# A four-part transformer kernel: last stage rearranged, and unread matrix products in the waits of the matrix engine

## The chip, the core and the metric

The kernel runs on one core of one Trainium2 chip. It is one program with an instruction stream for each engine: TensorE (PE) for matrix products, VectorE (DVE) and ScalarE (ACT) for elementwise work, GpSimd (POOL) for elementwise work and for scattering rows by indirect DMA, and SyncE (SP) for issuing the other DMAs. The engines run beside each other and are held together by semaphores alone. The metric is the device time of one execution in microseconds (us): the median over several.

## What is computed

An input x of 2 x 2048 tokens with 512 features, all float32, passes four residual blocks, each ahead of it with a layer norm without weights:

```python
x = x + rope_attention(norm(x), context)            # cross attention, 16 heads of 64, tanh-capped scores, 128 keys
x = x + quantised_ffn(norm(x))                      # weights and activations rounded to 8 bits; scale = max|x| over the whole tensor
x = x + masked_attention(norm(x), context)          # 16 heads of 32, 128 keys, masked scores set to 1e-9
x = x + routed_experts(norm(x))
def routed_experts(x):
    probs = softmax(x @ Wg + bg)                    # 512 columns
    idx = argmax(probs); p = max(probs); e = idx % 8
    return relu(x @ We[e] + be[e]) * p              # one of 8 experts for each token
```

The FFN needs the largest magnitude of its whole input before it can round the first value, and that of its whole hidden tensor before the product with w_down.

## The kernel before

The 4096 tokens are 32 tiles of 128 rows, in 8 groups (chunks) of 4 tiles (TPC = 4). x stays in SBUF as `xres`, 32 tiles of 512 float32. A float32 product is made as three products of rounded parts: hi x hi, lo x hi and hi x lo, where hi is the value rounded to a shorter float and lo = value - hi. Rounding to hi is ACT's, the subtraction for lo is DVE's (POOL's for the expert weights).

**Start of the rope attention (L441 to L600).** DVE normalises the context as soon as it has landed (L524 to L532), PE turns it (L580), ACT applies gain and shift (L491), and PE multiplies it with the key weights (L588). DVE rotates the results (L546 to L551) with a table that comes by DMA.

**Into the quantised stage.** The last products of the attention are followed by 44 transposes of weights in bf16 (L217). DVE finds the largest normalised magnitude (L921 to L1015), PE spreads it over the partitions with one product (L1209), DVE makes scales of it (L1017 to L1026), ACT scales x (L1285), DVE rounds (L1318, L1320), PE transposes (L1354) and makes the first small gate and up products (L1362), then the large ones (L1380).

**Down block.** Again a peak (DVE L1479, PE L1545, DVE L1481 to L1485), then ACT scales the hidden tensor (L1457) and DVE rounds it (L1493, L1495), in pieces (the lists FIRST, A_PIECE and D_PIECE), and PE multiplies (L1548).

**Masked attention (`first_step` and `body`, L2050 to L2120).** A written order of DVE's steps: `x_low` (L1971, low part of a turned row), `take_tops` (L1986, maxima of the scores, ahead of ACT's exponentials), `mask_scores` (L1980), `norm_row` (L1965), `invert` (L1996), `attn_low` (L2006), and in the last step `gate_top` (L2612 to L2617), the best of the 512 router columns. `gate_constants` (L2589 to L2597) sets small tables for the router. In tile 0 of a step PE's order is set by `first_step`.

**Routed experts (class ExpertStage, from L2360).** t counts tiles: t = 0 to 31 are router tiles (GATES = 32), t = 32 to 70 are slots (SLOT_TILES = 39), j = t - 32. For a router tile PE turns the normalised row (L2782), ACT rounds it (L2539) and DVE takes the low part (L2603, `take_lo`), PE makes 12 products with the router weights (L2792 to L2794), DVE finds the best column (L2612, L2614), ACT sums exponentials (L2545), and at the end of a group `hot` makes a one-hot of the experts (L2622 to L2629), PE ranks the tokens (L2805 to L2815) and `places` turns ranks into row numbers (L2634 to L2640). POOL's `scatter_rows` (L2486, L2493) writes the group's 4 tiles to DRAM sorted by expert. When 6 groups (EARLY) are counted, `tile_count` (L2646 to L2657), `tile_ends` (L2662 to L2668) and `tile_table` (L2678 to L2691) say which expert and which row each of the first 17 slots has (FULL_TILES); after all 8 groups the same is made for the other 22. For a slot, SP loads 128 sorted rows (L2434, `load`; 8 buffers; from j = 4 on after scatter(6)), PE turns them and makes 12 products with the expert's weights (L2835 to L2837), DVE adds the bias (`add_bias`, L2729) and applies relu, probability and residual (`finish`, L2733 to L2737), and POOL's `scatter_out` (L2500) writes the rows back by token. The weights of the 8 experts come early; ACT rounds them (`weights_high`, L2551), one 128 x 512 piece at a time, 4 for each expert, in the tiles that `pieces` names; the buffer of the rounded ones is that of x in part, so that a piece of group g waits for scatter(g). POOL makes their low parts (`weights_low`, L2478, L2484). In POOL's list, two low parts of expert e stand ahead of scatter(e - 1), two behind. Rows of sorted tiles that no token fills are written by SP (L2441, L2447).

Each engine takes its own instructions strictly in the written order: DVE's order within a tile t is add_bias of the slot before, take_lo of the next tile, finish, places, and then whatever extra work the list assigns to that t.

## Time and profile before

| | |
|---|---|
| median of 3 executions | 1476.54 us (1476.39 to 1477.39) |
| profiled execution | 1474.24 us |
| its span, first to last instruction | 1472.4 us |
| PE busy | 1416.4 us, 96% |
| DVE busy | 1194.5 us, 81% |
| ACT busy | 863.6 us, 59% |
| POOL busy | 524.1 us, 36% |
| mean granted clock of TensorE | 0.992 |

Busy is the time in which an engine had an instruction of its own under way. The granted clock is given as a share of the full 2.4 GHz; 0.50 is 1.2 GHz. In rows of the timeline, "x4" stands for four instructions in a row that are shown as one, and the bracket gives the time for which the engine was idle before, with the instruction or DMA that ended the wait. "issue" means that nothing in the profile explains it. A float32 product of 128 columns is two records.

### The profile page before, as it was taken

What the parts mean: (1) busy time and instruction counts of PE and PEld (TensorE: products, weight loads), DVE (VectorE), ACT (ScalarE), POOL (GpSimd) and SP (SyncE); (2) the same over time, 40 slices, a digit from 0 to 9 for tenths busy, and PEclk for the clock granted to TensorE, in tenths of its full rate; (3) what the DMA queues carried; (4) which work ended last, traced back from release to release, by engine and by line L of the source; (5) the groups of instructions that cost most, each with busy time, mean ns of one, the idle gap of its engine ahead of it and who ended that gap; (6) DMA issues with size and microseconds to landing.
All of it is one profiled execution on the core that took longest, in us unless ns stands there. A gap on an engine that the chain in (4) does not pass through costs nothing. (4 is left out here: it accounts for less than half of the span.)

```text
span 1472.4 us, 30141 instructions
## 1 busy us (share of the span) xinstructions
PE 1416.4 (96%) x10478; PEld 1061.3 (72%) x10478; DVE 1194.5 (81%) x2582; ACT 863.6 (59%) x2056; POOL 524.1 (36%) x511
## 2 busy tenths in 40 slices
PE   7999999999999999899998999999999999998996
PEld 5777777777777777644443467888888877776885
DVE  6778888787887865589988969999999997786775
ACT  2544444444444444655547848999999886773432
POOL 0122222222222222200003747655656655764333
PEclk9999999999999999999999999999999999999999
DMA  8511111110111102134415710000000026226641
GB/s 302 187 48 46 46 46 46 46 42 8 38 37 37 53 8 79 30 104 177 166 64 233 303 42 3 4 2 3 3 3 4 4 87 229 87 92 201 192 155 54
DMA packets 68658, 122.03 MB, mean 83 GB/s; under 512 B 30398, under 2 KB 36926, under 8 KB 67008
## 3 DMA queue, kind: packets, MB, share of 16 engines
q1 hardware_dynamic: 62864, 103.71, 20.8%
q0 software_dynamic: 5680, 16.85, 2.9%
q8 instruction: 66, 1.08, 0.3%
q14 instruction: 48, 0.39, 0.1%
HBM read 77.46 MB, written 39.80 MB: 80 GB/s over the span
## 5 line engine op out<-in xcount | busy, mean ns | idle before, releaser
L1840 ACT ACTIVATE c_probs<-c_score,c_minus_top 128x128 f32<-128x128 f32 x512 | 181.2, 381 | 27.2 <-DVE c_minus_top L1986 24.8
L1778 POOL TENSOR_TENSOR c_probs<-c_probs,c_recip 128x512 f32<-128x512 f32 x128 | 140.5, 1101 | 128.8 <-DVE c_recip L1996 125.1
L700 POOL TENSOR_TENSOR a_attn_lo_parts<-a_attn,a_attn_hi_parts 128x512 fp32r<-128x512 f32 x64 | 80.6, 1293 | 200.5 <-ACT a_attn_hi_parts L762 200.5
L758 ACT COPY a_attn<-a_pv_ps 128x512 f32<-128x512 f32 x64 | 36.6, 572 | 145.3 <-PE a_pv_ps L1068 145.3
L1451 POOL TENSOR_TENSOR xres<-xres,b_delta 128x512 f32<-128x512 f32 x24 | 48.3, 2028 | 196.9 <-DVE b_delta L1508 196.9
L1840 ACT ACTIVATION_READ_ACCUMULATOR c_probs<-c_score,c_minus_top 128x1 f32 x512 | 113.0, 221 | 0.0
L430 PE MATMUL a_bank<-a_x_hi_parts,a_wq_hi 128*128 128x256 f32 x512 | 106.4, 289 | 0.4 <-PEq L445 0.3
L696 POOL TENSOR_TENSOR a_x_lo_parts<-a_x_full,a_x_hi_parts 128x512 fp32r<-128x512 f32 x30 | 38.0, 1290 | 192.9 <-ACT a_x_hi_parts L733 192.9
L430 PE MATMUL a_bank<-a_x_lo_parts,a_wq_hi 128*128 128x256 f32 x512 | 102.3, 281 | 0.0
L430 PE MATMUL a_bank<-a_x_hi_parts,a_wq_lo 128*128 128x256 f32 x512 | 102.2, 281 | 0.0
L727 ACT ACTIVATE a_x_full<-a_bank,a_shift,a_gain 128x256 f32<-128x256 f32 x60 | 30.2, 555 | 119.4 <-PE a_bank L422 119.4
L1036 PE MATMUL a_bank<-a_wo_hi,a_attn_hi_parts 128*128 128x512 f32 x248 | 99.4, 401 | 0.0
L1038 PE MATMUL a_bank<-a_wo_hi,a_attn_lo_parts 128*128 128x512 f32 x248 | 98.1, 396 | 0.0
L1037 PE MATMUL a_bank<-a_wo_lo,a_attn_hi_parts 128*128 128x512 f32 x248 | 98.0, 395 | 0.0
L2539 ACT CAST d_xT_hi<-c_score 128x512 fp32r<-128x512 f32 x67 | 39.3, 586 | 98.2 <-PE c_score L2782 90.1
L1304 ACT ACTIVATE b_silu<-b_gate,ahead_scale 128x512 f32<-128x512 f32 x88 | 60.2, 684 | 61.7 <-PE b_gate L1380 61.1
L742 ACT ACTIVATE a_probs<-a_score_ps 128x1024 f32<-128x1024 f32 x64 | 65.6, 1025 | 41.2 <-PE a_score_ps L1053 41.2
L1380 PE MATMUL b_up<-b_xT,ahead_upT 128*128 128x512 bf16 x348 | 89.3, 379 | 0.0
L1380 PE MATMUL b_gate<-b_xT,ahead_gateT 128*128 128x512 bf16 x348 | 89.3, 379 | 0.0
L1980 DVE COPY_PREDICATED_SCALAR c_score<-c_masks,c_tiny 128x512 f32 (+1 forms) x96 | 89.1, 928 | 0.0
L430 PEld LDWEIGHTS a_bank<-a_x_hi_parts,a_wq_hi 128*128 128x128 f32 x512 | 78.3, 188 | 14.2 <-issue 6.3
L1986 DVE TENSOR_REDUCE c_minus_top<-c_score 128x4 f32<-128x512 f32 (+1 forms) x96 | 83.4, 869 | 3.2
(352 smaller groups left out, 4234.2 us busy)
## 6 DMA issues: line engine op xcount, KB each, us to landing
hidden<-b_hidden SPq DMA_DIRECT2D x5, 2816.0 KB, 8.3
b_hidden<-hidden SPq DMA_DIRECT2D x5, 2816.0 KB, 11.9
xres<-in_x SPq DMA_DIRECT2D x8, 1024.0 KB, 14.2
d_we<-in_we SPq DMA_DIRECT2D x8, 1024.0 KB, 6.7
xres<-in_w_gate_up SPq DMA_DIRECT2D x7, 1024.0 KB, 5.3
d_got<-rows SPq DMA_DIRECT2D x20, 258.0 KB, 2.9
xres<-rows SPq DMA_DIRECT2D x19, 258.0 KB, 2.7
a_rot<-in_rot SPq DMA_DIRECT2D x16, 256.0 KB, 3.0
```

The lines of the kernel that those rows point to most:

```text
L430: last = nc.tensor.matmul(out[:, i, :], w[:, k, cols], x[:, k, :], start=(j == 0 and i == 0), stop=(j == len(products) - 1 and i == 1))
L700: nc.gpsimd.tensor_tensor(of_spread(attn_lo, g), of_spread(attn, g), of_spread(attn_hi, g), ALU.subtract).then_inc(attn_lo_ready, 1)
L742: nc.scalar.activation(buf, score_ps[:, p % 2], ACT.Tanh, scale=1.0 / (DH0 ** 0.5 * GROK)).then_inc(capped, 1)
L1036: nc.tensor.matmul(out, hi, w_hi, start=first, stop=False)
L1037: nc.tensor.matmul(out, hi, w_lo, start=False, stop=False)
L1038: return nc.tensor.matmul(out, lo, w_hi, start=False, stop=last)
L1304: nc.scalar.activation(silu[:, u % RING, :], gate_ps[:, u % RING, :], ACT.Silu, scale=gate_scale[:, i:i + 1]).then_inc(silu_ready, 1)
L1380: last = nc.tensor.matmul(ps[:, u % RING, :], w[:, k, i * P:(i + 1) * P], xT[:, n % 2, k, :], start=(k == 0), stop=(k == KB - 1))
L1778: nc.gpsimd.tensor_tensor(part, part, recip[:, t % 2, heads].unsqueeze(2).to_broadcast([P, QUADS, KEYS]), ALU.mult).then_inc(scaled, 1)
L1840: last = nc.scalar.activation(probs[:, t, at, :], score_ps[:, h, g, :], ACT.Exp, bias=minus_top[:, h, g:g + 1], accum_out=total[:, t, at:a ...
L1980: ch.step(nc.vector.copy_predicated(part, masks[:, j, t, :].unsqueeze(1).to_broadcast(shape), tiny[:].unsqueeze(2).to_broadcast(shape)))
L1986: nc.vector.tensor_reduce(minus_top[:, PIECES[i]].rearrange("p h g -> p (h g)"), part, AX.X, ALU.max, negate=True).then_inc(top_ready, 1)
```

## The change

A helper `keep_busy` issues products of 128 x 128 float32 whose results nobody reads; it is called at ten places of PE's list. In the masked attention `gate_constants` moves into the first step, and in tiles with a gate `norm_row` moves behind `gate_top`. In ExpertStage POOL scatters a group's rows ahead of the low parts of the next expert; the two last low parts of the last expert go to DVE; the last group's four scatters are issued one by one behind the outputs of slots 4 to 7; counting takes three operations instead of five, and the tables are cut into `tile_passed`, `tile_experts` and `tile_rows`, spread over more tiles; SP fills unused rows later; the last slot is made in two halves of 256 columns. Cut to its core:

```diff
+
+
+def keep_busy(nc, out, square, times):
+
+    for _ in range(times):
+        nc.tensor.matmul(out, square, square, start=True, stop=True)
...
+            zeros, zeros_set = ctxT[:, 0, 0:P], sem("zeros_set")
+                    nc.vector.memset(zeros, 0.0).then_inc(zeros_set, 1)
+                    pe.wait_ge(zeros_set, 1)
+                    keep_busy(nc, ring.at(0)[:, 0, 0:P], zeros, 21)
...
+                pe.wait_ge(freed["dve"], last_out.emptied[1])
+                keep_busy(nc, peak_bank[:, 1, 0:P], ident[:], 4)
                 pe.wait_ge(ahead.peak_ready, 1)
-                pe.wait_ge(freed["dve"], last_out.emptied[1])
                 nc.tensor.matmul(peak_bank[:, 0, 0:P], row_scale[:, 0:1].to_broadcast([P, P]), ident[:], start=True, stop=True).then_inc(ahead.peak_turned, 1)
+                pe.wait_ge(ahead.taken, ahead.GROUPS_AHEAD + 1)
+                keep_busy(nc, score_ps[:].rearrange("p u h c -> p (u h c)")[:, 0:P], ident[:], 7)
...
+                    keep_busy(nc, up_ps[:, RING - 1, 0:P], ident[:], 11)
                     turn_first(0)
                     for t in range(1, TPC):
...
+                    pe.wait_ge(silu_ready, CHUNKS * IT - 2)
+                    keep_busy(nc, gate_ps[:, (CHUNKS * IT - 3) % RING, 0:P], ident[:], 6)
...
+                    keep_busy(nc, out_ps[:, BANKS - 2, 0:P], ident[:], 6)
                     pe.wait_ge(peak_ready, 1)
...
+                    keep_busy(nc, out_ps[:, BANKS - 2, 0:P], ident[:], 7)
                     pe.wait_ge(ld_down, 16 * KB)
...
+                                if q == 1 and t == 0 and i == A_PIECE.start:
+                                    keep_busy(nc, out_ps[:, g, 0:P], ident[:], 4)
                                 if t == 0 and i == A_PIECE.start:
                                     pe.wait_ge(whole_by_act, q)
...
+                    pe.wait_ge(out_freed, TPC * (CHUNKS - 1) - BANKS + TPC + 1)
+                    keep_busy(nc, out_ps[:, (TPC * (CHUNKS - 1) - BANKS + TPC) % BANKS, 0:P], ident[:], 5)
...
                     find_tops(1, 0, 1, 0)
                     find_tops(1, 0, 1, 1)
                     mask_scores(1, 0, 1, 2)
+                    gate_constants()
                     x_low(2 * NT, 0, 0, use(0, 0, 0, "T").out)
                     take_tops(2)
                     invert(1, 1, 0)
...
                         second = isinstance(n, int) and tile == 1
-                        if second:
-                            gate_constants()
...
-                        if s["N"]:
+                        if s["N"] and "L" not in s:
                             norm_row(tile + 2 * NT + 1, (t + 1) % 2)
                         if "L" in s:
                             dve.wait_ge(bank_full, gate_use[t].full)
                             gate_top(t)
+                            if s["N"]:
+                                norm_row(tile + 2 * NT + 1, (t + 1) % 2)
...
+        FILL = G + 3
+        LAST_SLOT, HALVES = SLOT_TILES - 1, (slice(0, D // 2), slice(D // 2, D))
...
+            if t // TPC == 2:
+                return {0: (), 1: (), 2: (0, 1), 3: (2, 3)}[t % TPC]
             return {0: (), 1: (0, 1), 2: (2,), 3: (3,)}[t % TPC]
...
+                sp.wait_ge(scattered, 16 * TPC * 2)
                 sp.dma_start(be[:].rearrange("p e n -> p (e n)"), io["be"].partition_broadcast(P)).then_inc(ld_be, 16)
                 for j in range(G):
                     load(j)
-                sp.wait_ge(no_row_set, 2)
-                sp.dma_start(io["rows"][NO_ROW:NO_ROW + P, :], no_token[:]).then_inc(filled, 16)
-                sp.wait_ge(behind_ready, 1)
                 for j in range(G, SLOT_TILES):
                     load(j)
-                    if j - G < EXPERTS:
-                        first = sp.value_load(behind_u[0:1, j - G:j - G + 1], min_val=0, max_val=NO_ROW - P)
-                        sp.dma_start(io["rows"][bass.ds(first, P), :], no_token[:]).then_inc(filled, 16)
+                    if j == FILL:
+                        sp.wait_ge(no_row_set, 2)
+                        sp.dma_start(io["rows"][NO_ROW:NO_ROW + P, :], no_token[:]).then_inc(filled, 16)
+                        sp.wait_ge(behind_ready, 1)
+                    for e in range(2 * (j - FILL), 2 * (j - FILL) + 2):
+                        if 0 <= e < EXPERTS:
...
-                if e >= 1 and k < 2:
+                if e >= 1 and k < 2 and e != EARLY:
                     pool.wait_ge(out_full, done(TPC * e))
-                elif e >= 1:
+                elif 1 <= e < EXPERTS - 1:
                     pool.wait_ge(hot_ready, e + 1)
                 nc.gpsimd.tensor_tensor(we_lo[:, e, k], we[:, e, k], we_hi[:, e, k], ALU.subtract).then_inc(we_lo_ready, 1)
...
-                for e in range(1, EXPERTS):
-                    for k in range(2):
+                for e in range(1, EXPERTS - 1):
+                    scatter_rows(e - 1)
+                    for k in range(KB):
                         weights_low(e, k)
-                    scatter_rows(e - 1)
-                    for k in range(2, KB):
-                        weights_low(e, k)
-                scatter_rows(GROUPS - 1)
+                for k in range(2):
+                    weights_low(EXPERTS - 1, k)
+                scatter_rows(GROUPS - 2)
                 for j in range(SLOT_TILES):
                     scatter_out(j)
+                    if TPC <= j < 2 * TPC:
+                        scatter_rows(GROUPS - 1, range(j - TPC, j - TPC + 1))
...
-                        for k in pieces(t):
+                        for k in pieces(t) if t < GATES - 2 else ((2, 3), ())[t - GATES + 2]:
                             weights_high(t // TPC, k)
...
-                ch.step(nc.vector.tensor_copy(counts[:], counted(i)))
-                ch.wait()
-                ch.step(nc.vector.tensor_scalar(whole[:], counts[:], float(add), None, ALU.add))
-                ch.wait()
-                ch.step(nc.vector.tensor_copy(whole_i[:], whole[:]))
+                ch.step(nc.vector.tensor_scalar(whole_i[:], counted(i), float(add), None, ALU.add))
...
-                    return x.unsqueeze(1).to_broadcast([1, n, EXPERTS])
                 dve.wait_ge(rstd_ready, len(DEVIATIONS))
                 ch.wait()
-                ch.step(nc.vector.tensor_tensor(passed[:, 0:n], each(ends[:]), place.unsqueeze(2).to_broadcast([1, n, EXPERTS]), ALU.is_le))
+                ch.step(nc.vector.tensor_tensor(passed[:, 0:n], ends[:].unsqueeze(1).to_broadcast([1, n, EXPERTS]),
+                                                place.unsqueeze(2).to_broadcast([1, n, EXPERTS]), ALU.is_le))
 
+            def tile_experts(j0, n):
+                ch.step(nc.vector.tensor_scalar(tile_expert[:, j0:j0 + n], expert_of[:, 0:n], float(EXPERTS - 1), None, ALU.min))
+
+            def tile_rows(j0, n):
-                ch.step(nc.vector.tensor_copy(tile_expert[:, j0:j0 + n], expert_of[:, 0:n]))
+                ch.step(nc.vector.scalar_tensor_tensor(row_of[:, 0:n], row_of[:, 0:n], origin[:, 0:1], ahead.table("slot", 1)[:, 0:n], ALU.add, ALU.add))
                 ch.wait()
-                ch.step(nc.vector.tensor_scalar(row_of[:, 0:n], row_of[:, 0:n], float(NO_ROW), None, ALU.min))
+                nc.vector.tensor_scalar(tile_row[:, j0:j0 + n], row_of[:, 0:n], float(NO_ROW), None, ALU.min).then_inc(tables_ready, 1)
+            def early_ends():
+                tile_ends(whole[0:1], ahead.table("first_row", 1))
+
+            def early_taken():
+
+                first = ahead.table("first_row", 1)
                 ch.wait()
...
             def rows_behind():
-                ch.step(nc.vector.tensor_tensor(behind[:], counts[0:1], ahead.table("first_row", 1), ALU.add))
-                ch.wait()
-                nc.vector.tensor_copy(behind_u[:], behind[:]).then_inc(behind_ready, 1)
+                nc.vector.tensor_tensor(behind_u[:], counted(1)[0:1], ahead.table("first_row", 1), ALU.add).then_inc(behind_ready, 1)
...
+            def last_low():
+                for k in range(2, KB):
+                    at = EXPERTS - 1, k
+                    dve.wait_ge(we_hi_ready, KB * EXPERTS - KB + k + 1)
+                    nc.vector.tensor_tensor(we_lo[:, at[0], k], we[:, at[0], k], we_hi[:, at[0], k], ALU.subtract).then_inc(constants, 1)
+
+            def expert_number(j):
+                return dve.value_load(tile_expert[0:1, j:j + 1], min_val=0, max_val=EXPERTS - 1)
...
                     if t == TPC * EARLY + 1:
                         tile_count(0, 0)
                     if t == TPC * EARLY + 2:
                         early_ends()
+                        tile_passed(FULL_TILES)
                     if t == TPC * EARLY + 3:
-                        tile_table(0, FULL_TILES)
-                    if t == GATES + 1:
+                        tile_experts(0, FULL_TILES)
+                        tile_rows(0, FULL_TILES)
+                    if t == GATES - 1:
+                        last_low()
+                    if t == GATES + 2:
+                        early_taken()
+                    if t == GATES + 3:
                         no_row()
-                    if t == GATES + 2:
+                    if t == GATES + 4:
                         tile_count(1, P - 1)
                         rows_behind()
-                    if t == GATES + 3:
+                    if t == GATES + 5:
                         late_ends()
-                    if t == GATES + 4:
-                        tile_table(FULL_TILES, REST_TILES)
-                add_bias(SLOT_TILES - 1)
-                finish(SLOT_TILES - 1)
+                    if t == GATES + 6:
+                        tile_passed(REST_TILES)
+                        tile_experts(FULL_TILES, REST_TILES)
+                    if t == GATES + 7:
+                        tile_rows(FULL_TILES, REST_TILES)
+                for half in range(len(HALVES)):
+                    add_bias(LAST_SLOT, number, half)
+                    finish(LAST_SLOT, half)
...
+                for half, cols in enumerate(HALVES if j == LAST_SLOT else (slice(0, D),)):
+                    if half == 1:
+                        out = logit_place(t + 1)
+                        pe.wait_ge(y_used, j - RING + 2)
+                    for k in range(KB):
+                        if j == 0 and k >= 2:
+                            pe.wait_ge(constants, CONSTANTS + k - 1)
+                        elif j == 0:
+                            pe.wait_ge(we_lo_ready, KB * (EXPERTS - 1) + k + 1)
+                        hi, lo = xT_hi[:, t % 2, k, :], xT_lo[:, t % 2, k, :]
...
```

Half 1 of the last slot is handled by `add_bias` and `finish` in the same way as a whole slot, and `scatter_out` of the last slot waits for both halves.

## Rows read from the trace of the kernel before

**Rows 1.** Windows: stretch, length, busy us (count) by engine, PEclk, DMA share, GB/s

```profile
619.00:625.50 6.50, 4.20 (x38) 3.76 (x39) 3.32 (x8) 4.89 (x9) 0.00 (x0) 0.50 0.73 159
...
779.00:786.00 7.00, 4.77 (x12) 1.92 (x13) 5.51 (x12) 5.42 (x5) 0.00 (x0) 0.51 0.00 0
...
1332.00:1336.00 4.00, 4.00 (x23) 3.10 (x24) 1.23 (x2) 1.15 (x2) 0.00 (x0) 0.57 0.76 239
...
1358.60:1461.00 102.40, 102.38 (x507) 83.77 (x504) 80.31 (x160) 39.57 (x61) 37.84 (x65) 1.00 0.48 153
```

**Rows 2.** Timeline of PE: start, us, line, operation; turns and waits of slots

```profile
1307.71 0.60 PE L2782 MATMUL c_score<-ident,c_xn 128*128 128x128 f32 x4
...
1330.75 0.49 PE L2835 MATMUL c_bank<-d_we_hi,d_xT_hi 128*128 x1 [1.96 <-POOL d_we_lo L2484]
...
1349.81 0.66 PE L2782 MATMUL c_score<-ident,c_xn 128*128 128x128 f32 x4 [1.69 <-ACT c_xn L2532]
...
1358.22 0.60 PE L2782 MATMUL c_score<-ident,c_xn 128*128 128x128 f32 x4
...
1454.81 0.60 PE L2782 MATMUL c_score<-ident,c_xn 128*128 128x128 f32 x4
```

**Rows 3.** The start: timelines of PE and DVE, and the view of line 588

```profile
8.39 1.09 PE L580 MATMUL a_bank<-ident,a_ctx 128*128 128x128 f32 x4 [8.39 <-DVE a_ctx L532]
...
L588 PE MATMUL a_bank<-a_ctxT,a_wk_or_wo x64: 379/379/792, 11.6 to 26.7; 128*128 128x256 f32 x64
...
13.90 0.17 DVE L536 TENSOR_SCALAR a_pad_bias<-a_pad_u 128x2 f32<-128x2 uint8 x1 [5.66 <-DMA a_pick<-in_pick]
```

**Rows 4.** Timeline of PE behind the peak of the rope attention

```profile
621.11 0.61 PE L1354 MATMUL b_bank<-ahead_ident,b_whole_x 128*128 128x128 bf16 x4 [3.69 <-DVE b_whole_x L1320]
```

**Rows 5.** Timeline of PE in the down block

```profile
796.02 4.49 PE L1548 MATMUL b_out<-b_downT,b_whole_h 128*128 128x512 bf16 x20 [1.07 <-DVE b_whole_h L1495]
```

**Rows 6.** Timelines of PE and DVE around the first step

```profile
902.88 1.10 PE L2220 MATMUL c_bank<-ident,c_probs 128*128 128x128 f32 x8 [0.87 <-DVE c_x_lo_parts L1971]
...
897.23 0.17 DVE L2589 MEMSET d_ones<- 128x128 bf16 x1
...
899.08 0.06 DVE L2597 MEMSET d_origin<- 1x1 f32 x1
```

**Rows 7.** Timelines of PE and DVE around the first gate of the last step

```profile
1207.26 0.66 PE L2155 MATMUL c_bank<-ident,c_xn 128*128 128x128 f32 x4 [1.54 <-ACT masked_bv L2545]
...
1203.32 1.42 DVE L1965 TENSOR_SCALAR c_xn<-xres,c_mv,c_rstd 128x512 f32<-128x512 f32 x1
```

**Rows 8.** Timelines of ACT and PE around the first scatter

```profile
1252.85 1.14 ACT L2551 CAST d_we_hi<-d_we 128x512 fp32r<-128x512 f32 x2 [3.12 <-DMA rows<-xres,d_slot_u]
...
1255.24 0.66 PE L2782 MATMUL c_score<-ident,c_xn 128*128 128x128 f32 x4 [1.50 <-ACT c_xn L2532]
```

**Rows 9.** Timelines of DVE and POOL at the end of routing

```profile
1304.57 1.21 DVE L2653 CAST d_whole_i<-d_whole 128x8 int32<-128x8 f32 x1
...
1342.04 0.17 DVE L2653 CAST d_whole_i<-d_whole 128x8 int32<-128x8 f32 x1
...
1304.46 2.55 POOL L2484 TENSOR_TENSOR d_we_lo<-d_we,d_we_hi 128x512 fp32r<-128x512 f32 x2 [1.67 <-ACT d_we_hi L2551]
...
1329.35 2.49 POOL L2484 TENSOR_TENSOR d_we_lo<-d_we,d_we_hi 128x512 fp32r<-128x512 f32 x2 [1.35 <-DVE d_onehot L2629]
...
1339.63 0.96 POOL L2493 DMA_INDIRECT rows<-xres,d_slot_u  x1 [0.30 <-issue]
```

**Rows 10.** Timelines of ACT and of the queue of SP

```profile
1348.45 0.59 ACT L2539 CAST d_xT_hi<-c_score 128x512 fp32r<-128x512 f32 x1 [5.49 <-remote]
...
1330.65 3.64 SPq L2434 DMA_DIRECT2D xres<-rows  x4
```

**Rows 11.** Timelines of DVE and POOL behind the last product

```profile
1461.19 0.69 DVE L2729 TENSOR_TENSOR d_y<-c_score,d_be 128x512 f32<-128x512 f32 x1 [0.84 <-PE c_score L2837]
...
1463.94 0.99 POOL L2500 DMA_INDIRECT out<-d_y,d_token_u  x1 [0.53 <-issue]
```

65 lines of the change are left out of this document (30 added, 35 removed).

## Prediction

> **What bounds the kernel now.** I read the table of busy times first, then the windows, then PE's waits, then the timelines around each of them. PE is the bound: where nothing disturbs it, it is busy 102.38 of 102.40 us at full clock [rows 1]. Its time falls only by filling or removing waits, by removing stretches at half clock, or by shortening what lies behind its last product. So each edit is costed by the wait of PE that it touches. A slot or gate tile has a natural period: from the turn at 1358.22 to that at 1454.81 there are 30 tiles, (1454.81 - 1358.22) / 30 = 3.22 us. From the turn at 1307.71 to that at 1358.22 there are 12 tiles in 50.51 us [rows 2]. Twelve periods are 38.64, two bundles of ranking products take some 0.35 together, so about 11.5 us are lost there: more than anywhere else, and it is where most edits aim.
>
> **Part 1, the start.** PE begins at 8.39, when the normalised context is there, and runs at half pace: four products of the 128x128 form take 1.09 us there and 0.60 later [rows 2, 3], and L588 has 792 ns as its longest and 379 as its median [rows 3]. The 21 unread products run before 8.39 and cover an idle engine. Each is two records 0.11 apart, so 0.22 us at full pace and 0.44 at half pace. With some 5.6 us at half pace (about 12.7 of them) and the rest at full pace, 21 take 7.4 us; from about 0.9 they end near 8.3. What follows, two turnings and the first 16 products, then saves 0.5 + 0.5 + some 1.4 = 2.4 us on PE. But DVE can't start on the products before 13.90, when a table that it reads first has landed [rows 3], and its blocks are a little longer than PE's, so that from there DVE sets the pace. About half of the saving lies behind 13.90 and reaches the stage: **+1.15** (a gain; 0 to 1.4, and -1.0 if all 21 run at half pace: 9.2 us, ending 1.7 after 8.39).
>
> **Part 2, into and out of the quantised stage.** PE waits 3.69 us for the first rounded x [rows 4] and then transposes and multiplies at half clock until about 625.5 (granted 0.50 over this stretch [rows 1]). The four products ahead of the peak (0.9 us) lie in PE's wait for the row scales and delay nothing, as long as it is that long. The 7 and 11 behind it take 18 x 0.22 = 4.0, up to 8 at half clock: they would end up to 0.5 us behind 621.11, and in return the transposes (0.61 for four [rows 4]) run at full clock. Behind these the chain over ACT and DVE is next, which caps the gain: **+0.5** (-0.2 to +0.9). In the down block PE works 4.77 of 7 us at half clock [rows 1]; 6 products ahead of the peak product push it back by 0.7 to 1.0, the 7 behind it make the first products fast. But PE stands again at 796.02, 1.07 us, for DVE's rounding [rows 5], which starts from the peak: the fast products only lengthen that wait. **+0.1** (-0.9 to +0.4). The 5 at the end lie in PE's wait for the next stage, already at full clock: 0.
>
> **Part 3, constants and the gate.** The block from 897.23 to 899.08 + 0.06 is 1.9 us of DVE [rows 6]. It moves ahead of x_low and the tops in the first step, and a softmax and the low part stand behind it. PE's wait of 0.87 for that low part at 902.88 [rows 6] starts from a stretch in which DVE has little slack, so 0.6 of 1.9 comes out: **-0.6** (-1.3 to 0). At 1207.26 PE waits 1.54 for ACT, which waits for the gate's best value; ahead of it on DVE stands the normalisation, 1.42 us long [rows 7]. With gate_top first that goes from this chain, and the masked scores are next after some 0.7 to 1.0: **+0.85** (0.5 to 1.2). The next normalised row comes 1.5 later and has cover in the product run behind it.
>
> **Part 4, scatters ahead of low parts.** PE waits 1.50 at 1255.24 for ACT's normalised row, and ACT stands 3.12 before it on a rounding of weights that waits for the rows of the first scatter [rows 8]. Two low parts of 1.27 us each had stood ahead of the four row scatters of 1.26 (0.96 + 0.30) [rows 9]. The scatter now starts 2.5 us earlier and the roundings for this group one or two tiles later: **+1.5** (1.0 to 1.5). SP's load of the bias is delayed past two groups, nobody needs it before the first slot.
>
> **Part 5, the end of routing and the first slots.** The 11.5 us divide like this. (a) 1.5 before the tile at 1312.43: in the counting an operation on integers took 1.21 us, and its neighbour as much, where the same took 0.17 with POOL elsewhere; POOL ran two subtracts from 1304.46 in the same 2.5 us [rows 9]. After: POOL is scattering there, three operations instead of five. (b) 1.0 at the next tile, where the table of slots, in one piece on DVE, held the last one-hot; now it is in three tiles. (c) 2.2 for the low parts of the last expert: POOL starts them at 1329.35 behind the one-hot, 2.49 us [rows 9], and PE gets them at 1330.75 after 1.96 [rows 2]. Now DVE does two of them (a subtract there is 0.6), and the other two stand ahead of the group's scatter. (d) 1.7 at half clock right after this wait (0.57 over 1332 to 1336 [rows 1]). (e) the rest, 5.1, in slots 3 to 7: ACT stood 5.49 [rows 10] and PE 1.69 at 1349.81 [rows 2]; the second table on DVE held the low part of the next slot; and there are shorter gaps.
> What the new order puts up against it. POOL: low parts of group 6 wait for its one-hot (about 1314) and take 5.1, two of the last 2.5, then scatter(6) runs to about 1327 and lands 2.6 later, about 1329.5; load(4) needs it. Before, SP issued load(4) at 1330.65 [rows 10]; slot 4 now comes up to 6 us earlier, near 1333.6, less 2.9 for the load: a second of slack. In slots 4 to 7 POOL has 0.18 + 0.53 + 0.99 for the output [rows 11] and 1.26 + 0.2 for one row scatter, 3.0 to 3.2 of 3.22: it just fits, and nothing reads its results within 15 us. DVE in a slot has 3.0 with the table pieces at most 1.0 more: three tiles now carry some 0.3 each of a wait. ACT's 5.49 is not released by any operation of the trace; the change does nothing against it. It cost PE about 2.3 (the 1.69 and what the turn had to make up), and I keep half. So 11.5 - 1.2 - 0.7 = **+9.6** (6.5 to 11.5).
>
> **Part 6, the last slot.** DVE's chain behind the last product is 0.69 + 0.49 + 0.69 from 1461.19, then POOL [rows 11]. Halved, the first half runs under PE's second and three operations of 256 columns (some 0.42) stay: **+0.7** (0.5 to 0.8).
>
> **The Trainium skill.** The row first: the integer operation took 1.21 beside POOL's subtracts, of 1.27 each [rows 9]. "SBUF — State Buffer", section "Who interferes with whom", says that a VectorE operation in a two-port form, or with two SBUF inputs, and a GpSimd operation lock each other out for a whole instruction; this trace agrees. By this rule the subtracts given to DVE could each cost one POOL operation, some 1.3 instead of 0.6, if POOL still runs low parts then; it would take 1.3 off Part 5 (inside its range). "TensorE: Matmul & The Clock Gate", Part 1, says that the point at which the clock rises shifts between executions of one kernel: no single trace here can show it.
>
> **The sum.** 1.15 + 0.5 + 0.1 - 0.6 + 0.85 + 1.5 + 9.6 + 0.7 = 13.8 us. The profiled execution had 1474.24 us (span 1472.4), so a profile of after should read 1460.4 at best guess; the runs have a median of 1476.54, 2.3 more, and 1462.7. I take off 0.8 for unread products that overrun their wait by one each: **1463.5**.
>
> **Rivals.**
> A. *Everything holds and ACT's stall goes too.* It needs the stall to be a matter of the order of work; 1.2 + 0.7 + 0.8 more: 1460.8. For it: waits of this length are nowhere else on ACT. Chance 0.17.
> B. *A new wait takes the old one's place.* Slot 4 has a second of slack and POOL 0.0 to 0.2 per slot; if scatter(6) lands 2 us later than reckoned, PE stands 1 us and, as at 1330.75, half clock follows (1.7), and the table pieces cost 0.3 more in three tiles: 3.6 back, 1467.1; with the lock above 1468.4. Chance 0.19.
> C. *Unread products don't do what they are for.* If reads of zeros or of one bank leave the clock at half, Parts 1 and 2 give nothing and the down block loses 0.9: 1.75 + 0.9 = 2.65 less, 1466.1. Against: the clock is granted in stretches with short 128-column products too. Chance 0.11.
> D. *Slower.* A per-slot gap that brings the clock down each time: POOL's queue of output and row scatter in slots 4 to 7. Half clock costs 3.2 us per slot, and the wait that brings it down some 2, so 5.2 a slot; the four slots are 21, and the result is 1463.5 + 21 = 1484.5. It decides from the third slot on (13.0 are to be lost, 15.6 would be). It needs POOL's slot to be 2 us longer than its rows say. Chance 0.03.
> E. *It doesn't shift the bound.* If the pieces of DVE's work only move its waits from tile to tile, Part 5 keeps (c) and (d) alone, 3.9, and Part 3 costs 1.3: 1463.5 + 5.7 + 0.7 = 1470. With C's loss 1472.5, and within 0.2% of before only with a further 1.5. Chance 0.05, of which half ends within 0.2%.
>
> **Chances.** Forecast 0.45, A 0.17, B 0.19, C 0.11, D 0.03, E 0.05. About 0.2% (3 us) is what measuring this kernel can tell from no change: faster 0.93, same 0.04, slower 0.03. The range has to leave out D, E and the ends of A and B: 1459.0 to 1469.0.
>
> **What would show it.** Right: PE's first products at 8.4 in the four-in-0.6 form; granted clock near 1.00 over 1330 to 1336; turns 3.2 to 3.6 apart throughout routing and slots; no wait at 1255; last chain of 0.42-us operations. Wrong: a wait of PE at slot 0 or 4 with POOL or DMA as releaser; half clock behind any unread products; POOL busy all through slots 4 to 7; the peak product of the down block over 0.7 later with the products behind it no faster. The number fails if Part 5 gives under 6.5, since all other parts together are 4.2.

## The result and the profile after

The changed kernel takes 1459.07 us (median of 5, 1458.48 to 1459.82), the kernel before 1476.39 (median of 5, 1474.45 to 1477.39): ratio 0.9881, 95% interval 0.987 to 0.9892, 17.3 us faster. The forecast was 1463.5, with 1459.0 as the lower end. The profiled executions stand closer together than the medians: 1474.24 and 1459.25, spans 1472.4 and 1457.4, so 15.0. The forecast for the profiled pair was 13.0: the parts add up to 13.8, less 0.8 for overruns, so a profiled execution of 1461.2.

Busy times of after, from its page, and its windows (stretch, length, busy us and count for PE, PEld, DVE, ACT, POOL, granted clock, DMA share, GB/s):

```profile
PE 1424.8 (98%) x10610; PEld 1076.6 (74%) x10632; DVE 1193.1 (82%) x2579; ACT 864.1 (59%) x2056; POOL 521.5 (36%) x512
```

```profile
619.00:625.50 6.50, 5.43 (x65) 4.94 (x66) 3.32 (x8) 5.18 (x8) 0.00 (x0) 1.00 0.79 159
776.00:783.00 7.00, 5.50 (x44) 4.83 (x43) 4.82 (x14) 2.24 (x3) 0.00 (x0) 1.00 0.01 2
...
1300.00:1332.00 32.00, 31.77 (x173) 25.77 (x172) 29.22 (x89) 21.57 (x41) 18.08 (x19) 1.00 0.47 149
1332.00:1336.00 4.00, 4.00 (x21) 3.28 (x20) 3.27 (x10) 1.41 (x3) 1.18 (x2) 1.00 0.67 199
```

The stretches at half clock [rows 1] are all at full clock now (while PE has work, this trace is below it only over 8 to 16 us, 0.87 and then 0.71), and PE works 31.77 of 32 us at the end of routing. Its timeline, as far as it answers [rows 2 to 5 and 7]:

```profile
1.05 6.39 PE L272 MATMUL a_bank<-a_ctxT 128*128 128x128 f32 x42 [1.05 <-DVE a_ctxT L529]
8.35 0.63 PE L590 MATMUL a_bank<-ident,a_ctx 128*128 128x128 f32 x4 [0.90 <-DVE a_ctx L540]
...
619.04 2.69 PE L272 MATMUL b_up<-ident 128*128 128x128 f32 x22 [0.35 <-PEq L647]
621.57 0.61 PE L1367 MATMUL b_bank<-ahead_ident,b_whole_x 128*128 128x128 bf16 x8
...
778.13 1.58 PE L272 MATMUL b_out<-ident 128*128 128x128 f32 x12 [0.61 <-PEq L1274]
779.54 0.39 PE L1562 MATMUL b_out<-ident,b_peak 128*128 128x128 f32 x2
...
794.15 6.21 PE L1565 MATMUL b_out<-b_downT,b_whole_h 128*128 128x512 bf16 x28 [1.16 <-ACT b_whole_h L1487]
```

L272 is the unread product. The same points in both traces, with how much earlier after is:

| point | before | after | earlier |
|---|---|---|---|
| first large gate product | 626.30 | 626.01 | 0.29 |
| first turned row of the masked attention | 870.35 | 869.33 | 1.02 |
| last turn ahead of the gate | 1195.07 | 1193.65 | 1.42 |
| turn behind the 1.54 us wait | 1207.26 | 1204.55 | 2.71 |
| turn behind the first scatter | 1255.24 | 1250.88 | 4.36 |
| turn at 1307.71 [rows 2] | 1307.71 | 1303.32 | 4.39 |
| turn ahead of slot 0 | 1326.80 | 1319.58 | 7.22 |
| turn of slot 1 | 1333.71 | 1323.20 | 10.51 |
| turn at 1358.22 [rows 2] | 1358.22 | 1343.07 | 15.15 |
| last turn | 1454.81 | 1439.98 | 14.83 |
| last scatter | 1463.94 | 1448.91 | 15.03 |

### The profile page after: what moved, and what is told of

The parts are those of the page before. It is cut to its first block and busy times, and to the rows that moved or that the text cites. A ratio compares the mean times of both kernels' runs of the same rounds, so it can differ in the third digit from the quotient of the medians.

```text
span 1457.4 us, 30436 instructions
## 1 busy us (share of the span) xinstructions
PE 1424.8 (98%) x10610; PEld 1076.6 (74%) x10632; DVE 1193.1 (82%) x2579; ACT 864.1 (59%) x2056; POOL 521.5 (36%) x512
```

## The experiments

Every run is named with the median of the kernel before that was measured beside it. The executions of before were timed anew for each group of runs, with medians between 1476.28 and 1477.87; after was timed once, beside 1476.39. The single times of after lie within 1.3 us, those of most of its variants within 0.8 to 3 and those of e3 within 4.3, mostly with four executions each. So a difference of two medians under about 1 us is not read; stretches of a trace compare more closely, but each shows one execution.

**Twice the same.** The kernel before, unchanged.

> The kernel before, unchanged. Question: the forecast for the profiled execution (1459.6 to 1460.4) came out (1459.25), but the medians moved by 17.3 us and the profiled executions by 15.0. Theory S (spread): single executions of before scatter by about 3 us (1474.45 to 1477.39), the profiled one was at the low end, and a second profile lies between 1474 and 1477.5, with its excess in waits that come and go (ACT's unexplained 5.49 us wait, the clock's half stretches). Theory P (profile): profiling before costs nothing or helps, and a second profile is again 2 us under the median of its timed runs.

Measured 1476.91 (1474.19 to 1479.62, 11 executions); 15 more of the same kernel beside them 1477.05 (1473.06 to 1479.02). This time the profiled execution was the median one. Its windows:

```profile
864.00:868.00 4.00, 3.37 (x13) 2.60 (x12) 2.40 (x10) 2.96 (x5) 1.12 (x2) 0.58 0.76 265
1208.00:1212.00 4.00, 2.77 (x13) 2.78 (x14) 3.45 (x10) 2.93 (x7) 1.04 (x1) 0.67 0.81 234
1332.00:1336.00 4.00, 1.99 (x10) 1.18 (x11) 0.79 (x2) 1.11 (x3) 2.50 (x2) 0.96 0.30 86
1336.00:1340.00 4.00, 4.00 (x25) 3.44 (x24) 2.70 (x7) 1.30 (x2) 0.00 (x0) 0.61 0.72 197
1352.00:1356.00 4.00, 3.49 (x10) 2.69 (x11) 3.66 (x13) 1.75 (x3) 1.20 (x2) 0.59 0.71 174
```

Three more stretches at half clock than in the trace that the forecast was made from, each behind a wait of PE of 1.5 to 1.9 us (1.78 ahead of 864, 1.53 ahead of 1209, 1.91 ahead of 1352). Mean granted clock 0.989 against 0.992. Of the 26 executions, 21 have 0.988 to 0.990 and a mean of 1477.3 us, 5 have 0.991 or 0.992 and a mean of 1475.5 (1473.06 to 1477.06). Theory S holds. Between these two traces what comes and goes is for the larger part the clock. From the down block's peak product to the masked attention's first turn, across the fall at 864, this trace takes 92.73 us and the first one 91.35. From the turn behind the 1.5 us wait to the first turn of the last stage, across the fall at 1208, it takes 18.28 against 17.31. That is 2.4 of the 2.7 by which it ends later. But clock and time don't go together in every single execution (one with 0.992 took 1477.06), so that other things scatter too.

**The unread products.** The helper is called at nine places (not ten, as the section on the change has it), for 71 products. In e2 it does nothing; e6, e7 and e8 take them out at one place, e17 at the end of the down block.

```diff
 def keep_busy(nc, out, square, times):
-    for _ in range(times):
-        nc.tensor.matmul(out, square, square, start=True, stop=True)
+    return                                             # e2
-keep_busy(nc, ring.at(0)[:, 0, 0:P], zeros, 21)
+keep_busy(nc, ring.at(0)[:, 0, 0:P], zeros, 0)         # e6; likewise e7: 4, 7, 11; e8: 6, 6, 7, 4; e17: 5
```

> After without any unread product (the calls stay, the helper does nothing). By the forecast's terms the unread products are worth 1.15 + 0.5 + 0.1 = 1.75 us less 0.8 of overrun: 1460 to 1461. By the two traces: 0.3 at the start, 0 into the quantised stage, about 0.7 from there to the masked attention: 1.0, so 1460.1. Theory K (the unread products steady the clock in timed runs as well): over 2 us, above 1461.5, with a wider scatter of its single times than the 1.3 us of after.

> After without the 21 unread products at the start. Forecast: 1.15 slower, 1460.2. Theory D from the traces: the first results are only 0.3 us earlier in after, because DVE's first rotation waits for a table: 1459.4, within the scatter of after.

> After without the 22 unread products between the rope attention and the quantised stage. Forecast: 0.5 slower. The traces: the first large product starts equally late against the stage's end in both kernels (626.30 - 613.20 = 13.10 and 626.01 - 612.90 = 13.11), so 0: 1459.1. Theory K (they also keep the clock from falling later or in other executions): over 1 us slower, with a lower mean clock.

> After without the 23 unread products around and in the down block (the 5 at its end stay). Forecast 0.1 slower. The traces: 0.7 us gained between 776 and 870, so 1459.8. Theory K: the drop in clock behind the peak can be followed by another at the stage's end in some executions: 1461 and more, mean clock 0.993 to 0.995.

> After without the 5 unread products at the end of the down block. They fill 1.1 of PE's 1.8 us wait for the masked attention. Theory K2: without them this wait brings the clock down in some executions, as one trace of the kernel before and the one without any unread product show just there (0.58 and 0.63 over four us, costing about 1.5 us); so some executions at 1459, some at 1460.5, median 1459.5 to 1460.3, wider scatter. Forecast: 0, since in the profiled execution of before the clock stayed up: 1459.1.

| run | us | before | mean granted clock |
|---|---|---|---|
| after | 1459.07 | 1476.39 | 0.996 to 0.998 |
| e2, none | 1463.03 (1462.91 to 1464.8) | 1477.05 | 0.991 |
| e6, none at the start | 1460.63 (1460.01 to 1461.27) | 1477.49 | 0.997, 0.998 |
| e7, none into the stage | 1459.45 (1459.04 to 1459.79) | 1477.49 | 0.994, 0.995 |
| e8, none in the down block | 1459.15 (1458.02 to 1460.12) | 1477.49 | 0.994 to 0.996 |
| e17, none at its end | 1459.65 (1458.89 to 1460.85) | 1476.98 | 0.996, 0.997 |

All together give 4.0 us, four times the 0.95 that the forecast had left for them; the start alone 1.6, the others singly 0.1 to 0.6, which medians can't tell from nothing. Theory D is wrong. At the start, PE's timeline in e6, the same in after, and DVE's in e6:

```profile
11.34 9.00 PE L598 MATMUL a_bank<-a_ctxT,a_wk_or_wo 128*128 128x256 f32 x27 [0.66 <-ACT a_ctxT L498]
```

```profile
11.03 5.34 PE L598 MATMUL a_bank<-a_ctxT,a_wk_or_wo 128*128 128x256 f32 x16 [0.66 <-ACT a_ctxT L498]
```

```profile
18.01 0.42 DVE L554 TENSOR_TENSOR a_keysT<-a_bank,a_rot 128x256 f32<-128x256 f32 x1 [1.15 <-PE a_bank L598]
```

In e6 the half pace lasted into the second block, so that DVE waited for PE twice: 1.78 us for the first, and 1.15 more in the last line. In the trace of before it ended earlier and DVE waited once [rows 3]. The table that DVE waits for lands between 13.2 and 14.7 us from one execution to the next. With the unread products DVE begins within 0.1 us of that, in 12 of the 15 traces that have them (in after's own and two more the clock fell for a moment before the work began); in the five traces without them it begins at 15.05 to 15.49. At the rope attention's end this is 1.5 us: its first transpose of weights comes at 612.38 in the mean of the 15 and at 613.86 in the mean of the five. The pair of before and after shows only 0.3 of it (613.20 and 612.90). At the end of the down block (e17, then after), windows again:

```profile
864.00:868.00 4.00, 4.00 (x14) 3.32 (x14) 3.25 (x7) 1.40 (x2) 0.56 (x1) 0.72 0.85 312
```

```profile
864.00:868.00 4.00, 3.96 (x18) 3.52 (x19) 2.92 (x7) 2.45 (x3) 0.85 (x2) 1.00 0.99 350
```

Theory K2 holds for this trace: without the 5, the next 24 products take 6.92 us instead of 5.45. The forecast had given them nothing. The clock fell in the profiled execution, the slowest of four (1460.85); the other three took 1458.89 to 1459.89.

**Shorter runs of them.** 1 instead of 6 ahead of the peak, 8 instead of 11 ahead of the transposes.

```diff
-keep_busy(nc, up_ps[:, RING - 1, 0:P], ident[:], 11)
+keep_busy(nc, up_ps[:, RING - 1, 0:P], ident[:], 8)
-keep_busy(nc, out_ps[:, BANKS - 2, 0:P], ident[:], 6)   # the one ahead of the peak product
+keep_busy(nc, out_ps[:, BANKS - 2, 0:P], ident[:], 1)
```

> After with 1 unread product instead of 6 ahead of the down block's peak product, and 8 instead of 11 ahead of the first transposes. The traces show the peak product at 779.54 where its input was there at 778.43, and the first transposes at 621.57 where theirs was at 620.76. If the clock stays up, 0.8 to 1.0 faster at the peak and 0 to 0.5 at the transposes: 1457.6 to 1458.3. Rival: the shorter runs let the clock fall behind the peak, as without any in the down block, and what is gained is lost: 1459.1.

Measured 1457.56 (1456.6 to 1458.3, before 1476.98; ratio 0.9871, 0.9852 to 0.989): 1.5 under after, the fastest kernel of the study.

```profile
777.28 0.49 PE L1562 MATMUL b_out<-ident,b_peak 128*128 128x128 f32 x2
777.61 1.73 PE L272 MATMUL b_out<-ident 128*128 128x128 f32 x14
780.01 9.93 PE L1565 MATMUL b_out<-b_downT,b_whole_h 128*128 128x512 bf16 x44 [0.67 <-DVE b_whole_h L1511]
```

The peak product comes 152.69 us behind the first large gate product (777.28 - 624.59), against 153.53 in after, and the products behind it are at full clock: 1 does as well as 6 there, and the other 5 delayed the chain by 0.8. The first large gate product comes 12.40 us behind the first transpose of weights, against 12.9 to 13.1 in the traces with 11: there too the run was too long. Whole stretches, in us, one trace each:

| | first transpose of weights to peak product | peak product to first turn of the masked attention |
|---|---|---|
| before | 165.80 | 91.35 |
| after | 166.64 | 89.79 |
| e7, none into the stage | 166.85 | 89.78 |
| e8, none in the down block | 165.60 | 91.38 |
| e17, none at its end | 166.64 | 91.27 |
| e18, shorter runs | 165.09 | 89.89 |
| e2, none | 166.31 | 93.33 |

So the products in the down block save 1.6 us behind the peak and cost 1.0 ahead of it, the 5 at its end save 1.5 in this trace, and those into the stage save 0.2, since their length costs what the clock gives. e18 keeps the savings without most of the cost.

**The two moves in the masked attention.** e3 has the expert stage's edits alone; e4 puts the constants back, e5 the normalisation.

```diff
                     mask_scores(1, 0, 1, 2)
-                    gate_constants()                   # e3, e4: back to tile 1
...
-                        if s["N"] and "L" not in s:    # e3, e5
+                        if s["N"]:
```

> After without unread products and with both moves in the masked attention undone: the expert stage's changes alone. By the traces the expert stage gives 1.7 at the first scatter, 10.8 to the slots and 0.6 at the last slot, less 0.7: about 12.3, so 1464.1. By the forecast's terms 1.5 + 9.6 + 0.7 = 11.8: 1464.6. If the extra 2.3 us of the medians belong to the expert stage (its wait for no visible reason), it is 14.5: 1461.9.

> After with the router's constants back in the second tile. Theory L (lock): the block costs what POOL beside it makes it cost; its two casts take 0.22 and 0.12 us in the new place and about 0.8 each in the old, and the move is worth 0.5 to 0.8 us: 1459.6 to 1459.9. Rival M (forecast): the block costs 1.9 wherever it is, the move cost 0.6: 1458.5.

> After with the normalisation ahead of the gate's best again. The traces show the turn after PE's 1.54 us wait 1.27 us earlier in after than the turns before it: theory G says the move is worth that 1.2 to 1.3 us, 1460.3, and the wait is back. By the forecast 0.85: 1459.9. If in the old place the wait also brings the clock down in some executions (it does in one trace of the kernel before, 0.67 over four us), then more, 1461 and a wider scatter.

e3: 1464.38 (1461.62 to 1465.95, before 1477.05). The expert stage alone gives 12.7, and both moves 1.35 (1464.38 - 1463.03 of e2), little against the 4.3 us over which the five executions of e3 scatter. e4: 1459.59 (1459.11 to 1460.12); e5: 1459.2 (1458.45 to 1459.94, three executions; a fourth took 4679.59 and is left out). Singly both are too small for medians, but the traces tell the mechanism. DVE in after, in e4, and in e5:

```profile
893.65 0.22 DVE L2625 CAST d_upper<-router_tables 128x128 bf16<-128x128 f32 x1
...
894.05 0.12 DVE L2628 CAST d_base<-router_tables 128x32 bf16<-128x32 f32 x1
```

```profile
895.89 0.82 DVE L2626 CAST d_upper<-router_tables 128x128 bf16<-128x128 f32 x1
...
896.89 0.78 DVE L2629 CAST d_base<-router_tables 128x32 bf16<-128x32 f32 x1
```

```profile
1200.57 0.55 DVE L1987 TENSOR_SCALAR c_xn<-xres,c_mv,c_rstd 128x512 f32<-128x512 f32 x1
```

POOL at this point in e5, then in before, and PE in e5:

```profile
1200.67 1.34 POOL L1800 TENSOR_TENSOR c_probs<-c_probs,c_recip 128x512 f32<-128x512 f32 x1
```

```profile
1203.42 1.04 POOL L1778 TENSOR_TENSOR c_probs<-c_probs,c_recip 128x512 f32<-128x512 f32 x1
```

```profile
1203.64 0.66 PE L2176 MATMUL c_bank<-ident,c_xn 128*128 128x128 f32 x4 [0.67 <-ACT masked_bv L2576]
```

The constants' block takes 0.6 us in its new place, where POOL is idle, and 1.9 in the old one, where POOL scales probabilities from 895.38 on. Theory L holds. The normalisation took 1.42 in the trace of before [rows 7] and takes 0.55 in e5 in the same place of DVE's list. A POOL operation begins 0.10 us behind its start in both; in before DVE's operation is drawn out, in e5 POOL's (1.34 instead of 1.04). PE's wait is 0.67 in e5 instead of 1.54, a difference of 0.87, which is that of the two durations. After's wait is 0.25, so against e5 the move is worth 0.4, not the 1.29 of the table (2.71 - 1.42): the other 0.87 is what the normalisation had lost to POOL in before. Why it lost it there (both traces of the kernel before have 1.42) and not in e5 stays open.

**The first scatter.** e9 restores POOL's order and the pieces of group 2, e13 SP's early load of the bias.

```diff
                 for e in range(1, EXPERTS - 1):
-                    scatter_rows(e - 1)
-                    for k in range(KB):
-                        weights_low(e, k)
+                    # e9: two low parts, scatter_rows(e - 1), two low parts (e = 6 as in after)
...
             def rest():
-                sp.wait_ge(scattered, 16 * TPC * 2)    # e13
```

> After with POOL's order of before for the experts 1 to 5 (two low parts, the scatter, two low parts) and the weight pieces of group 2 in their old tiles. Forecast and trace agree on 1.5 to 1.7 us: 1460.7, with PE's wait of 1.5 us behind the first scatter back. If the move matters beyond that wait (a fall of the clock behind it, or low parts on POOL beside DVE), over 2.5: 1461.6 and more.

> After with SP's load of the expert bias at its old time, ahead of the scatters (its wait for two scattered groups is taken out). Theory B: PE's 1.5 us wait behind the first scatter came from this load, whose 2 MB kept the DMA engines full so that the scatter landed 7.8 us after its issue; the order on POOL had no part in it, since putting the old order back cost nothing. Then the scatter lands late again: ACT's rounding of weights waits 1 to 3 us and PE up to 1.5, 1459.5 to 1460.6 (POOL's new order starts the scatter 2.8 us earlier, so part of the wait stays hidden). Rival (forecast): the order on POOL alone is what counted, and nothing changes: 1459.1.

e9: 1459.21 (1457.65 to 1460.59, before 1477.87), no wait of PE at this place in its trace. e13: 1460.82 (1459.67 to 1462.08, before 1476.28), 1.75 slower. So the wait of 1.5 us came from the bias load and not from POOL's order. In before SP issued the load at 1233.10, the DMA engines were 0.95 busy over 1232 to 1252, and the rounding resumed at 1252.85 [rows 8], when they were free:

```profile
1233.10 0.54 SPq L2437 DMA_DIRECT2D d_be<-in_be  x1
```

```profile
1232.00:1252.00 20.00, 20.00 (x111) 16.28 (x110) 17.32 (x60) 13.28 (x27) 11.05 (x14) 1.00 0.95 368
```

In e13 it goes another way, which no theory had. POOL, then DVE, then PE:

```profile
1250.56 0.19 POOL L2506 TENSOR_TENSOR d_held<-d_held 128x1 f32<-128x1 f32 x1 [4.45 <-DMA rows<-xres,d_slot_u]
...
1256.06 2.52 POOL L2514 TENSOR_TENSOR d_we_lo<-d_we,d_we_hi 128x512 fp32r<-128x512 f32 x2
```

```profile
1255.71 2.90 DVE L2654 TENSOR_SCALAR d_expert_i<-d_where 128x4 uint32<-128x4 uint32 x1
```

```profile
1259.10 0.19 PE L2855 MATMUL c_bank<-d_base,d_ones 128*128 128x32 bf16 x1 [1.80 <-DVE d_onehot L2661]
```

The late landing pushes the second scatter and the low parts behind it onto the end of a group, and DVE's operation on 4 integers, 0.17 elsewhere, ends only with POOL's second subtract.

**The end of routing and the slots.**

```diff
-                    if t == GATES - 1:                 # e11: the last two low parts on POOL,
-                        last_low()                     # ahead of scatter_rows(6)
...
+                scatter_rows(GROUPS - 1)               # e10: whole, ahead of the first output
...
-HALVES = (slice(0, D // 2), slice(D // 2, D))
+HALVES = (slice(0, D),)                                # e12
...
+                        tile_passed(FULL_TILES)        # e14: each table in one tile, 27 and 38
...
+                    # e15: low parts (6, 0) and (6, 1) ahead of scatter_rows(5)
+                    # e16: fills of unused rows right behind load(7)
```

> After with the last group's four scatters in one piece ahead of the first slot's output, as before. Theory F (ACT's unexplained wait of 5.2 to 5.5 us in slot 4 is a fetch of its instructions behind this burst of scatters and the loads): the wait comes back, PE loses about 2 us: 1461. Rival: the wait belonged to the place of the instruction in ACT's list against the loads; nothing comes back, and only the outputs of slots 0 and 1 are later: 1459 to 1459.5.

> After with the last expert's last two low parts on POOL, ahead of the scatter of group 6. They take 1.27 us each there and the scatter, so the load of slot 4, comes 2.5 us later. Forecast's thin second of slack at slot 4: 1.5 us slower, 1460.6. The trace of after shows the load of slot 4 issued at 1324.83, 8 us ahead of its use: then no loss, 1459.1, or 0.3 faster by the 1.28 us that DVE saves.

> After with the last slot in one piece. DVE's chain behind the last product is 0.69 + 0.49 + 0.69 again instead of three of 0.42, 0.35 and 0.42: 0.7 slower by the forecast, 1459.8; in the traces it is 463.94's chain: PE's last product to POOL's last scatter start 2.96 us before, 2.70 after, so only 0.3 at that end, and PE's 24 half products cost 0.4 more than 12 whole ones: then 0 to 0.3.

> After with each table of slots in one piece again, at the tiles where its largest part stands now. Forecast: 1.0 for the first and 1.45 for the second, 2.4 slower together: 1461.5. Rival R: the first has cover, since casts to integers and the counting are shorter (0.8 us less on DVE) and no other wait is left; only the second costs, 0.5 to 1: 1459.8.

> After with the first two low parts of expert 6 back ahead of the scatter of group 5, so that POOL subtracts while DVE counts. Theory L (DVE's operation on 8 integers waits for POOL's subtract): two of the three counting operations take 1.0 to 1.25 us instead of 0.16 to 0.20, and PE waits about 1.2 at the next tile: 1460.3. Rival: the shorter counting (3 operations) has taken the problem away: 1459.1.

> After with SP's writes of unused rows right behind the load of slot 7 again. Both traces of the kernel before show ACT standing 5.2 to 5.5 us in slot 4 with no releaser named, no trace with the new expert stage shows it, and putting the last scatter in one piece did not bring it back. Theory W: it hangs on SP's fills and the loads behind them at this time; it comes back and costs 1.5 to 2.5 us: 1461. Rival: it belonged to the old order of DVE's and POOL's work, nothing comes back: 1459.1.

| run | us | before |
|---|---|---|
| e10, last scatter whole | 1458.94 (1458.49 to 1459.92) | 1477.87 |
| e11, low parts on POOL | 1461.16 (1460.3 to 1462.47) | 1477.87 |
| e12, last slot whole | 1459.33 (1458.67 to 1459.78) | 1477.87 |
| e14, tables whole | 1459.9 (1459.35 to 1460.61) | 1476.28 |
| e15, low parts beside the counting | 1459.47 (1458.12 to 1459.86) | 1476.28 |
| e16, fills early | 1459.57 (1458.97 to 1459.78) | 1476.28 |

Only e11 is clearly slower, 2.1 us. Undone one by one, these edits cost 4.1 us in all, 2.1 of them e11's and the rest too small for medians, while the gain of this place is about 11. So the runs show what the stage's edits give together (e3), but not how most of it divides among them; the shorter counting was not undone at all. For that the traces alone speak, by the waits that are gone. ACT and PE in its trace:

```profile
1330.08 0.81 ACT L2565 ACTIVATE c_xn<-xres 128x512 f32<-128x512 f32 x1 [2.52 <-DMA xres<-rows]
```

```profile
1330.95 0.66 PE L2831 MATMUL c_score<-ident,c_xn 128*128 128x128 f32 x4 [1.24 <-ACT c_xn L2565]
```

The load of slot 4 is issued at 1326.88, behind the later scatter, instead of 1324.83. ACT wants it 3.3 us after after's issue (1328.09), and in e11 it waits until 1330.08, 3.2 us behind the issue: there was no second of slack, there was next to none, and my expectation's "8 us ahead" took PE's use for ACT's. e15 shows the lock again, 1.21 us for an operation on 8 integers:

```profile
1299.49 2.55 POOL L2515 TENSOR_TENSOR d_we_lo<-d_we,d_we_hi 128x512 fp32r<-128x512 f32 x2 [1.67 <-ACT d_we_hi L2589]
```

```profile
1299.39 0.17 DVE L2689 TENSOR_SCALAR d_whole_i<-d_whole_i 128x8 int32<-128x8 int32 x1
1299.60 1.21 DVE L2691 CAST d_whole<-d_whole_i 128x8 f32<-128x8 int32 x1
```

But only one of the three is caught and PE waits 0.25: with fewer operations in the way, the lock costs little there. ACT's wait of 5.2 to 5.5 us, found in both traces of the kernel before [rows 10], came back in none of e3, e10 or e16. Neither the last scatter in one piece nor the fills cause it; what does is open.

## Why the prediction was too high

**The step from the profile to the median failed.** It is the largest single part of the miss: 13.0 us were forecast (1476.54 - 1463.5) and 17.3 measured, 4.3 more, of which this step is 2.3 and the parts are 2.0. The parts put a profile of after at 1460.4, and at 1461.2 with 0.8 taken off the gain for overruns (e1's expectation took it off the time, 1459.6, which is wrong); it read 1459.25. To the 1460.4 I then added the 2.3 us by which the median of before lay over its profiled execution, as if it were a fixed cost. After has no such cost: its median and its profiled execution agree (1459.07, 1459.25). What the 2.3 is, e1 shows for one pair of traces: 2.4 of 2.7 us are half-clock stretches that the one execution had and the other had not. After's trace has no stretch of 4 us below full clock between 16 us and the end of PE's work, and its five executions have a mean clock of 0.996 to 0.998, so this part of before is gone as well; that it went by the filled waits is argued from these clocks and from e2, which has 0.991 and loses 4.0. A wait was priced by its length alone; its clock in other executions was not. The start scatters too: before's trace is 0.7 ahead there of the mean of its kind, after's 0.5 behind.

In the profiled pair the parts come out like this, by the table of points; that the first row fits is luck, since the pair shows 0.3 of the start's 1.5.

| | forecast | measured |
|---|---|---|
| Parts 1 and 2, less overruns | 0.95 | 1.02 |
| Part 3 | 0.25 | 1.69 |
| Part 4 | 1.5 | 1.65 |
| Part 5 | 9.6 | 10.8 |
| slots from 1358 on, and Part 6 | 0.7 | -0.1 |

**Part 1** (+1.15): nearly right in the mean, 1.5 over all traces and 1.6 by e6; the 0.3 of the profiled pair is the small end of its scatter.

**Part 2** (+0.5, +0.1, 0): singly 0.4, 0.1 and 0.6 in medians, each too small to be told from nothing; 0.2, 0.5 and 1.5 in the traces. The argument for the +0.1 was wrong: fast products behind the peak don't only lengthen the wait at 796.02, they shorten the stretch to the masked attention by 1.6 (91.38 in e8, 89.79 in after). The products at the end, put at nothing because this one execution kept its clock, are worth 1.5 where it falls. The deduction of 0.8 for overruns was right in kind and too small: the run ahead of the peak alone costs that, and e18 gets 1.5 back by shortening two runs.

**Part 3** (-0.6, +0.85): the sign of the first was wrong. I took 1.9 us of DVE along to the new place, where the block takes 0.6: the durations of its casts belong to POOL's work beside them. The second is 0.4 in e5, where the normalisation is short; in before the place cost 0.87 more. Together 1.35 by e2 and e3 and 1.69 in the pair, where 0.25 was forecast.

**Part 4** (+1.5): the size was right and the cause wrong. I passed over SP's late bias load with "nobody needs it" and looked only at what waits for it, not at what shares the DMA engines with it.

**Part 5** (+9.6): 10.8 in the traces (15.15 - 4.39), 12.7 for the expert stage in medians, less 1.5 to 1.75 for the first scatter 11.0. By the table, (a) and (b) gave 2.8 of 2.5 forecast, (c) and (d) 3.3 of 3.9, and (e) 4.6 where 3.2 had been kept (5.1 less 1.2 and 0.7). So the excess lies in (e): ACT's stall, of which half was kept, went. (b) and the second table are at most 0.8 together in e14, not 2.4: its trace shows no wait of PE over 0.23 from 1296 to 1350.

**Part 6** (+0.7): 0.3 at most by e12, too small for medians, and in the pair 0.2 from the last turn to the last scatter. DVE was still at the first half when the second arrived: its three operations and the token's end at 1446.92, PE's last product at 1446.2.

**Rivals.** A was the nearest, 1460.8, and the stall went, as it has it; that this is a matter of the order of work isn't shown. Its 1460.8 also contains the 2.3 and no overruns, so that it comes near in part by luck. B's mechanism is real, with slot 4 as its place (e11), but needs two POOL operations more than the change has. C is refuted by the clock of 1.00 over 619 to 625.5, and by that of e2, 0.991, against 0.997. D and E didn't come.

## What to carry to other kernels

Compare medians with medians: before a sum is made from one profile, look whether its mean clock is that of the other executions, and where any execution shows a wait of PE followed by half clock, price that wait with the 1 to 1.5 us that the stretch costs where other engines wait for PE behind it (e1, e17). Fill it with no more products than it holds: 1 did what 6 did, and 8 gave more than 11 (e18). Ask of a DVE operation that looks too long what POOL does beside it, before its time is carried to another place. And a large load that nobody is waiting for is not free if a small transfer that somebody waits for is under way.

## What the runs showed of the hardware

- Some DVE operations end with a POOL subtract or product under way: 0.17 becomes 1.21 (e15), 0.22 becomes 0.82 (e4), 0.55 becomes 1.42 [rows 7], and 0.17 becomes 2.90 where two POOL operations follow on each other (e13). Once it was POOL's that grew, 1.04 to 1.34 beside DVE's 0.55 (e5). Others beside the same POOL operations keep their length: in e4 the memset between the two casts takes 0.17. The Trainium skill, "SBUF — State Buffer", section "Who interferes with whom", says that the loser of the shared ports stands still for the other's whole instruction; these numbers agree.
- The same kernel with the same data has its clock fall at other places from execution to execution: mean granted clock 0.988 to 0.992 for the kernel before, with 1473.06 to 1479.62 us. The Trainium skill, "TensorE: Matmul & The Clock Gate", Part 1, says of the point where the clock rises that it shifts between executions of one kernel; what these runs show shifting is whether it falls, behind waits of 1.5 to 1.9 us (e1).
- At the start the record of the granted clock says 1.00 where products run at half pace (e6 over 14 to 18 us: 12 products in 4 us, later 20); there the durations tell the clock, not the record.
- A small table issued at the start lands at 13.2 to 14.7 us in the 20 traces. In the 12 in which DVE waits for nothing else the rope attention's end moves with it: 611.50 for a landing at 13.31, 612.77 for 14.61.
